# A gated cross-attention and feed-forward kernel on one core: feed-forward matrix summed and split at other times, three tiles turned in pieces, inputs loaded and measured earlier

## The reference

```
x   = x + tanh(g_xattn) * (attention(layernorm(x), ctx) @ Wo + bo)
x   = x + tanh(g_ffn)   * (layernorm(x) @ W[idx] + b[idx])

attention: q = layernorm(x) @ Wq, k = ctx @ Wk, v = ctx @ Wv, 16 heads of 64,
           softmax(q k^T / 8) v for each head
idx = argmax(log_softmax(logits) + gumbel(u))     # one of 8 matrices of 512 x 512
```

## Time and profile before

| | before |
|---|---|
| median of 3 runs | 1051.0 us (1050.85 to 1053.32) |
| the profiled execution | 1052.3 us, span 1050.5 us |
| PE busy | 1034.4 us (98%) |
| DVE busy | 851.6 us (81%) |
| ACT busy | 743.7 us (71%) |
| POOL busy | 438.9 us (42%) |
| mean granted clock of TensorE | 0.998 |

### The profile page before, as it was taken

One profiled execution on the slowest core, in us unless ns is written; L12 is line 12 of the kernel. 1 busy time (PEld: TensorE's weight loads), 2 busy tenths in 40 slices (PEclk: granted clock), 3 DMA queues, 4 the chain that ended last, 5 costly groups with the idle time before them and its releaser, 6 DMA issues.

```text
span 1050.5 us, 21819 instructions
## 1 busy us (share of the span) xinstructions
PE 1034.4 (98%) x6065; PEld 588.0 (56%) x6065; DVE 851.6 (81%) x1800; ACT 743.7 (71%) x2712; POOL 438.9 (42%) x635
## 2 busy tenths in 40 slices
PE   9998899999999999999999999999999999999998
PEld 7634455555555555555555555555555555555555
DVE  3867988888888887888888887888888887888876
ACT  3588887766776676767776677767776776767762
POOL 0575444444433343444433443444433443444322
PEclk9999999999999999999999999999999999999999
DMA  8413466656666656655666656655666656655655
GB/s 310 101 30 105 94 128 136 134 114 118 129 136 135 135 126 136 135 118 110 132 138 135 135 121 139 137 112 111 132 138 137 136 123 134 134 113 114 133 116 141
DMA packets 383639, 135.02 MB, mean 129 GB/s; under 512 B 361728, under 2 KB 363316, under 8 KB 383540
## 3 DMA queue, kind: packets, MB, share of 16 engines
q1 hardware_dynamic: 383476, 134.09, 59.0%
q0 software_dynamic: 64, 0.00, 0.0%
HBM read 27.48 MB, written 16.78 MB: 42 GB/s over the span
## 4 chain that ended last, share of the span: by engine, by line
PE 93%; DVE 3%; ACT 1%; DMA 1%; issue 1%; SPq 0%; POOL 0%; DVEq 0%
PE banks L1355 84%; PE banks L1579 3%; PE banks L1458 1%; PE banks L1385 1%; PE banks L1394 1%; PE banks L1466 1%; DVE vw_area L1062 1%; ACT vw_area L811 1%; PE banks L1447 1%; DMA fold_area<-in_ctx 1%; DMA work<-work 0%; ACT work L858 0%; DVE fold_area L1070 0%; DVE work L425 0%; DVE red L1153 0%
## 5 line engine op out<-in xcount | busy, mean ns | idle before, releaser
L858 ACT ACTIVATE work<-banks,red,cst 128x77 f32<-128x77 f32 x1024 | 409.1, 426 | 89.1 <-DVE red L1153 89.1
L1355 PE MATMUL banks<-fold_area,work 128*128 128x462 f16 (+1 forms) x2304 | 410.6, 336 | 1.4 <-DMA work<-work 0.7
L1355 PE MATMUL banks<-vw_area,work 128*128 128x512 f16 x1674 | 373.0, 380 | 2.6 <-DMA work<-work 2.6
L1355 PEld LDWEIGHTS banks<-fold_area,work 128*128 128x128 f16 x2304 | 223.9, 97 | 176.2 <-DMA work<-work 1.2
L1355 PEld LDWEIGHTS banks<-vw_area,work 128*128 128x128 f16 x1674 | 164.1, 98 | 188.4 <-DMA work<-work 2.9
L425 DVE SCALAR_TENSOR_TENSOR work<-work 128x256 f16<-128x256 f32 (+3 forms) x444 | 240.1, 575 | 3.8 <-ACT work L881 3.3
L858 ACT ACTIVATION_READ_ACCUMULATOR work<-banks,red,cst 128x1 f32 x1024 | 221.0, 216 | 0.0
L1151 DVE TENSOR_REDUCE stats<-banks 128x6 f32<-128x462 f32 (+1 forms) x192 | 112.0, 584 | 109.1 <-PE banks L1355 108.7
L1355 PE MATMUL banks<-work 128*128 128x256 f16 x1302 | 162.4, 272 | 1.6 <-DVE work L1236 1.6
L1355 PEld LDWEIGHTS banks<-work 128*128 128x128 f16 x1302 | 126.8, 98 | 33.1 <-DVE work L1236 2.2
L703 POOL TENSOR_TENSOR stats<-stats,cst 128x1 f32<-128x1 f32 x64 | 12.5, 195 | 283.8 <-DVE stats L1187 283.8
(11 more groups left out here) (145 smaller groups left out, 814.4 us busy)
## 6 DMA issues: line engine op xcount, KB each, us to landing
work<-in_x SPq DMA_DIRECT2D x64, 256.0 KB, 2.8
out<-work SPq DMA_DIRECT2D x63, 256.0 KB, 2.2
work<-work SPq DMA_TRANSPOSE x254, 3.1
fold_area<-in_L_xattn_Wo SPq DMA_DIRECT2D x4, 512.0 KB, 9.2
work<-in_L_ffn_W SPq DMA_DIRECT2D x2, 1024.0 KB, 7.0
fold_area<-in_L_xattn_Wq SPq DMA_DIRECT2D x2, 1024.0 KB, 12.9
fold_area<-in_L_xattn_Wk SPq DMA_DIRECT2D x2, 768.0 KB, 12.1
fold_area<-in_L_xattn_Wv SPq DMA_DIRECT2D x2, 384.0 KB, 6.8
```

Source lines behind the costliest of these rows:

```text
L858: nc.scalar.activation(probs_of(h, h + 1), s_bank(m, k)[:, (h - h0) * J:(h - h0 + 1) * J], ACT.Exp, bias=nmx[:, h:h + 1], scale=exp_scale, ...
L1355: mm = nc.tensor.matmul(ps, lhs(l), rhs(r), start=first and n == 0, stop=last and n == 2, skip_group_check=onto)
```

## The change

What it does, in the order of the program:

- SP: x of tiles 2 and 3 is loaded before x of tile 1 is turned, tiles 4 and 5 in step 1. From step 4 on, in all even steps and in the loop too, the turn of x comes ahead of the two loads, where it came behind them.
- The probabilities of tiles 1 and 2 are turned in four pieces too. The load of the feed-forward bias goes behind the turn of tile 1.
- POOL sums the quarters in step 0 ahead of x_scale of tile 2, from the first maxima on. In steps 1 to 4 its x_scale stands ahead of its other additions. The multiplication of the bias with its gate moves from ACT (step 2) to POOL (step 2).
- ACT splits three quarters ahead of the exponentials of tile 0, two behind its probabilities, two behind those of tile 1. DVE makes five low parts in step 1 and two in step 2, where it made three and four.
- DVE: x_moments of tile 2 in step 0 goes behind the first maxima; in steps 1 to 4 x_moments goes ahead of softmax, where it stood between the two pieces. x_low in steps 1 and 2 goes ahead of the third maxima.
- `xT_second` moves from slot 7 to slot 4.

```diff
-        xT_second = xr[:, RING - 1, :].bitcast(F16).rearrange("p (s k n) -> p s k n", s=2, k=KT)
+        xT_second = xr[:, RING // 2, :].bitcast(F16).rearrange("p (s k n) -> p s k n", s=2, k=KT)
...
-            return is_tile(o, m, 0, NT - 1)
+            return is_tile(o, m, 0, 1, 2, NT - 1)
...
+            for n in (2, 3):
+                load_x(0, n)
             sp.wait_ge(k_stage_lo, key_staged_before(UNITS))
             turn_x(0, 1)
...
+                    if valid(o1) and not is_tile(o, m, 0):
+                        turn_x(o1, m1)
                     for lag in (2, 3):
                         ol, ml = tile(o, m, lag)
-                        if valid(ol):
+                        if valid(ol) and not is_tile(o, m, 0, 2):
                             load_x(ol, ml)
-                    if valid(o1) and not is_tile(o, m, 0):
-                        turn_x(o1, m1)
...
+                    if is_tile(o, m, 1):
+                        sp.wait_ge(s_done, 2 * len(BANKS))
+                        for n in (4, 5):
+                            load_x(0, n)
...
-                    elif not early:
+                    elif not early or is_tile(o, m, 1, 2):
                         due(o_done, nth(o, m))
...
                 pool.wait_ge(wf_again, 16)
-                pool.wait_ge(p_lo, 4)
+                pool.wait_ge(nmx_ready, 1)
                 nc.gpsimd.tensor_tensor(t1, b12, b11, ALU.subtract).then_inc(wf_summed, 1)
                 pool.wait_ge(wf_summed, 1)
                 nc.gpsimd.tensor_tensor(b12, b22, b12, ALU.subtract).then_inc(wf_summed, 1)
-                pool.wait_ge(s_done, 2 * len(BANKS))
...
+                if is_tile(o, m, 1, 2, 3, 4):
+                    x_scale(on, mn)
                 if valid(o2):
                     if is_tile(o2, m2, 0):
+                        pool.wait_ge(bias_loaded, 16)
+                        pool.wait_ge(gate_ready, 1)
+                        nc.gpsimd.tensor_tensor(bias, bias, gates[:, 1:2].to_broadcast([P, D]), ALU.mult).then_inc(bias_ready, 1)
                         pool.wait_ge(bias_ready, 1)
...
                     nc.gpsimd.tensor_tensor(xr[:, m2, :], xr[:, m2, :], bias, ALU.add).then_inc(x2b_ready, 1)
-                if valid(on):
-
-                    x_scale(on, mn)
                 if is_tile(o, m, 0):
                     weights_summed()
+                if valid(on) and not is_tile(o, m, 1, 2, 3, 4):
+
+                    x_scale(on, mn)
...
+                if is_tile(o, m, 0):
+                    weights_high(AS_LOADED)
                 if grouped:
                     group_high_of(*pair, 2 if m % 2 == 0 else 0)
...
                 if is_tile(o, m, 0):
-                    weights_high(AS_LOADED)
+                    weights_high(AS_SUMMED[:2])
                 if is_tile(o, m, 1):
-                    weights_high(AS_SUMMED)
+                    weights_high(AS_SUMMED[2:])
...
+                if is_tile(o, m, 0):
+                    x_moments(on, mn)
+                    dve.wait_ge(x_stats, 3)
+                    x_variance()
...
                 if is_tile(o, m, 1):
-                    weights_low(AS_LOADED, 0)
+                    weights_low(AS_LOADED + AS_SUMMED[:2], 0)
                 if is_tile(o, m, 2):
-                    weights_low(AS_SUMMED, len(AS_LOADED))
+                    weights_low(AS_SUMMED[2:], len(AS_LOADED) + 2)
...
+                if is_tile(o, m, 1, 2, 3, 4):
+                    x_moments(on, mn)
+                    dve.wait_ge(x_stats, nth(on, mn) + 1)
+                    x_variance()
                 if valid(o):
                     softmax(o, m, 0)
...
-                if valid(on):
+                if valid(on) and not is_tile(o, m, 0, 1, 2, 3, 4):
                     x_moments(on, mn)
```

More of the change, by code:

```diff
@@ L564, in step @@
                     sp.dma_start_transpose(turned[:, start:, :], ps[:, start * P:]).then_inc(pT_turned, 16)
+                    if is_tile(o, m, 1):
+                        sp.dma_start(bias, ffn_b[bass.ds(op, 1), :].to_broadcast([P, D])).then_inc(bias_loaded, 16)
                 if is_tile(o, m, NT):
@@ L919, in weights_high @@
                 act.wait_ge(wf_again, 16)
+                act.wait_ge(k_stage_lo, len(STAGED_KEYS))
                 for i in places:
@@ L939, in step @@
                     exponentials(o, m, 1)
-                if is_tile(o, m, 2):
-                    act.wait_ge(bias_loaded, 16)
-                    act.wait_ge(gate_ready, 1)
-                    nc.scalar.activation(bias, bias, ACT.Copy, scale=gates[:, 1:2]).then_inc(bias_ready, 1)
                 if grouped:
@@ L1316, in step @@
                     maxima(o, m, 1)
+                if is_tile(o, m, 1, 2):
+                    x_low(o1, m1)
                 if valid(o2):
@@ L1320, in step @@
                     maxima(o, m, 2)
-                if valid(o1) and not is_tile(o, m, 0):
+                if valid(o1) and not is_tile(o, m, 0, 1, 2):
                     x_low(o1, m1)
                 if is_tile(o, m, 1):
-                    weights_low(AS_LOADED, 0)
+                    weights_low(AS_LOADED + AS_SUMMED[:2], 0)
                 if is_tile(o, m, 2):
-                    weights_low(AS_SUMMED, len(AS_LOADED))
+                    weights_low(AS_SUMMED[2:], len(AS_LOADED) + 2)
                 if multiplied:
@@ L1540, in attention @@
                 b, turned, early = m % B, probs_place(o, m), turned_early(o, m)
-                turns = 16 if is_tile(o, m, 0) else 32
+                turns = 16 * (number(o, m) + 1 if is_tile(o, m, 0, 1, 2) else 4) if early else 0
                 if early:
```

9 lines of the change are left out of this document (2 added, 7 removed).

## The result

The changed kernel takes 1056.2 us in the median of ten runs, against 1051.3 for the kernel before on the same chip: ratio 1.0049, 95% interval 1.0034 to 1.0064, so 3.6 to 6.7 us slower. The forecast was 1052.0, range 1048.7 to 1054.5. The profiled execution takes 1059.15 us (span 1057.3). This is the page's row of busy times after the change (answers to the earlier trace rows).

The account below looks back on a forecast made before the run. TensorE, busy 98%, bounds the kernel; at most 6.07 us of idle and clock could be won. About 4.5 won early is lost again, attention(4) starts 1.0 later: 1051.0 + 1.0 = 1052.0 us, range 1048.7 to 1054.5.

Parts of the forecast that it names:

- Slack 3.4 becomes 1.8: hidden: Loop, even steps: VectorE waits 1.6 us for late x loads; slack before attention(6) falls but covers it, costing nothing.
- Rival D: Loop, slower, chance 0.12: loads landing later than 4.6 us leave even steps uncovered, at 28 times the excess; 0.3 makes 1060.
- Tile 0: First step: GpSimd's sums beside VectorE's maxima delay attention(0) by 0.5 us; TensorE idle 1.7 instead of 1.16.
- Scores(2) and attention(1): First steps: idle of 0.73 and 2.62 and clock loss of 1.56 go; TensorE about 4.5 us ahead.
- Step 2, bias on GpSimd, +2.5: Step 2: GpSimd's two bias instructions take turns with VectorE's four low-part instructions of line 425, delaying VectorE 2.5 us.
- rival B: GpSimd's instructions hardly delay VectorE, chance 0.24: attention(4) 1.5 to 2.5 us earlier, time 1049.
- The stall of 3.2 before scores(4) and the fall of the clock, 1.6: Tile 4's x turned no earlier: TensorE idles 3.2 us before scores(4), then loses 1.6 to a lower clock.
- Step 4, +1.0: Step 4: tile 6's late load holds VectorE's moments, 3.5 us late, so attention(4) starts 1.0 us later, at about 164.5.

Follow-up runs that it names:

- experiment 4: Kernel before, with only the loop's loads of x (step 6 on) put behind the turn of x: 1053.21 us, ratio 1.0010.
- experiment 7: Changed kernel with five harmless one-element fills more on VectorE, long before the first scores: 1051.38 us, ratio 0.9987.
- 8: Kernel before with the loop's x loads behind the turn of x, plus harmless instructions ahead: ten SyncE, three GpSimd, two ScalarE; 1052.36 us, ratio 1.0000.
- experiment 3: Changed kernel with the loads of x ahead of the turn of x in all even steps, step 4 too: 1050.76 us, ratio 0.9993.
- experiment 10: Changed kernel with x loads ahead of the turn, bias multiplication back on ScalarE, bias loaded where the kernel before loads it: 1050.54 us, ratio 0.9982.
- experiment 5: Changed kernel with one harmless instruction more on ScalarE, a logarithm of four numbers far ahead of the loop: 1055.17 us, ratio 1.0028.

## Why the prediction was wrong

**The step that failed:** "Slack 3.4 becomes 1.8: hidden", in the loop. Three of its numbers were off.
- The slack was read at tile 6 and taken for all even steps. In the loop's first step, where the engines also pay for the loop's turn, it is 7.09 - 4.9 = 2.2 in the kernel before. It decides, since it is the smallest.
- VectorE's wait was 1.8 to 1.9 instead of 1.6. After it 0.2 to 0.5 is left, not 1.8 (5.00 - 4.8 in experiment 4, 5.37 - 4.9 in the changed kernel).
- The landing was taken as 4.9, the median of the earlier trace rows, whose longest is 6.5. I read the median and not when the long ones come. At this turn it was 5.8, because the change took five instructions from VectorE's program ahead of the loop (experiments 7 and 8). The prediction had no term and no rival for it.

The loss needs both, the late load and the late landing: with an early load the same 5.8 is hidden (experiment 3: issued 7.2 ahead, landed in 5.8, no stop), with a landing of 4.8 to 4.9 the late load is hidden (4, 7, 8).

**Rival D** named the place and the side, with a chance of 0.12, but not the condition: it asked for loads of x that land later than 4.6 us. They landed in 2.9 in the median (longest 5.6); the turn of probabilities was the late one. And its price, 28 times the excess, was too high: only the first tile of each of the seven turns of the loop stops, by 0.2 to 0.6.

**Tile 0:** right. Idle of 1.58 against a forecast of 1.7, shift +0.43 against +0.5.

**Scores(2) and attention(1):** right. Neither stops; attention(1) ends at 126.66, 33.2 us behind the first scores; before it was 37.9, so 4.7 ahead against 4.5.

**Step 2, bias on GpSimd, +2.5:** the mechanism was right, VectorE and GpSimd took turns; the size was 3.34 - 1.65 = 1.69. Of these only 0.72 us reach attention(4) (experiment 10 beside 3). The Trainium skill's exclusive lock ("SBUF — State Buffer", section "SBUF: two separate sides") agrees with these rows: VectorE's first low part took 1.58 us instead of 0.96 beside GpSimd's first instruction, GpSimd's second 1.86, and VectorE's second part, 1.38 instead of 0.31, ended 0.18 us behind it. This alternation decides against rival B, which needed VectorE to keep its turn.

**The stall of 3.2 before scores(4) and the fall of the clock, 1.6:** wrong. Tile 4's x is turned 136.99 - 93.45 = 43.54 us behind the first scores, before 45.82, so 2.3 us earlier: I had left it where it was. The stop came at attention(3) instead, 1.89, and the clock stayed up. So attention(3) had a shift of -1.70 where I had +0.2.

**Step 4, +1.0:** the mechanism was right, the sum not. These are the turn of x, the loads behind it, and VectorE's moments that wait.

```profile
149.89 1.23 SPq L462 DMA_TRANSPOSE work<-work  x1
151.18 1.38 SPq L470 DMA_DIRECT2D work<-in_x  x1
...
154.83 0.69 DVE L1009 BATCH_NORM_STATS2 stats<-work 128x6 f32<-128x512 f32 x1 [4.12 <-DMA work<-in_x]
```

The wait was 4.12 (2.5 by the forecast's own numbers, 152.95 - 150.44; its 3.5 has the moments themselves in it), and TensorE stopped 0.87 before attention(4). But it stood on the gain of the steps before, so the shift was -0.67 and not +1.0; without the late loads it is -1.77 (experiment 3).

Had only the first steps counted, the change would have been some 0.7 us faster, inside the range, though not by the forecast's sum. The error of -1.7 there and that of +4.0 in the loop have opposite signs; the second decided.

## What to carry to other kernels

Where a change eats slack in a loop, take the slack from the worst step of a turn of the loop (here the first, 2.2 instead of 3.4 us), and the landing from the long ones of that place, not from the median of all. When a stop comes and goes with edits that have nothing to do with it, look at the queues that load instruction code: here five one-element fills on VectorE were worth 3.3 us. An operation that is moved to GpSimd can hold up VectorE, and one that stays on ScalarE holds up what waits behind it: test both places, with the operand loaded early.

## What the hardware showed that I had not expected

- A turn of 20 blocks lands in 4.8 to 4.9 us, and in 5.6 to 6.5 in 21 of 29 cases in which a load of instruction code falls 3.75 to 4.6 us behind its issue; without one, in none of 29 (changed kernel). The data are hardly slower: at tile 14 the last packets moved 4.54 us behind the issue, against 4.38 in experiment 4, while the landing came at 5.8 and 4.8. In the 8 turns that a code load did not delay, the last packets were not late either (4.42 or less). Why 0.15 us at the packets become 0.9 at the landing stays open; it wasn't tried.
- Where an engine's code loads fall in a loop moved with the number of instructions ahead of it: five more on VectorE took one from 4.0 to at most 1.75 us behind tile 14's issue (experiment 7), one more on ScalarE took another from 1.75 away (experiment 5). With VectorE's five the loop's growth of the shift fell from 4.0 to 1.2 us, with the same work in it.
- After a stop of 2.00 us TensorE's granted clock fell (mean 0.62 over the next 4.5 us), after stops of 1.87 to 1.96 at the same place it did not, and in the trace of experiment 4 it did not after 2.40 before attention(1) either, where it fell after 2.54 to 2.62 in three other traces.
